# A vision layer on one core: row maxima taken over 256 keys straight into the FP16 stack, the stack's high parts written by ScalarE, the output division in one pass

## The reference

```python
h = _L0_tok_ref(x, L0_tok_W, L0_tok_b)
h = h + _L0_attn_ref(_layernorm(h, axis=-1), wq, wk, wv, wo)
h = h + _L0_ffn_ref(_layernorm(h, axis=-1), clip_x, clip_down, w_gate, w_up, w_down)
...
# attention, 16 heads of 16 features, 4 key/value heads, rotary positions
scores = jnp.einsum('bshd,bthd->bhst', q, k) * scale
scores = jnp.where(causal[None, None, :, :], scores, jnp.float32(-jnp.inf))
attn = jax.nn.softmax(scores, axis=-1)
out = jnp.einsum('bhst,bthd->bshd', attn, v).reshape(Bx, Sx, Dx)
return out @ wo
```

## Time and profile before

| | |
|---|---|
| median of 3 runs | 898.87 us (895.33, 898.87, 903.66) |
| span of the profiled execution, first to last instruction | 901.6 us |
| the profiled execution's own time | not listed apart; its span is 2.7 us above the median and within the runs |
| DVE busy over the span | 793.9 us (88%) |
| PE, POOL, ACT busy | 709.8, 537.5, 509.0 us |
| granted PE clock, mean | 0.938 of full |
| first stage | to about 724 us |
| second and third stage | about 724 us to the end |

### The profile page before, as it was taken

The page is one execution under the profiler, slowest core; times in us unless marked ns, Lnnn a source line. Parts: engine busy times, 40 slices in busy tenths (PEclk is TensorE's granted clock), DMA queues, the critical chain, the costliest instruction groups (busy, mean ns, idle before and its releaser), DMA issues. The chain is left out here.

```text
span 901.6 us, 21285 instructions
## 1 busy us (share of the span) xinstructions
PE 709.8 (79%) x6962; PEld 381.5 (42%) x6962; DVE 793.9 (88%) x1320; ACT 509.0 (56%) x748; POOL 537.5 (60%) x545
## 2 busy tenths in 40 slices
PE   3668788878888888888888888888786559996775
PEld 2444344444444444444444444444433223332453
DVE  6867688988999999999999999999996349998898
ACT  3324455555665565556655655565554438886664
POOL 1435666666777776677777766777753238882000
PEclk9686999999999999999999999999989769998999
DMA  7233445564554555555545555554544222223488
GB/s 255 64 70 84 99 106 117 119 126 103 132 119 108 120 118 120 122 128 134 119 108 120 118 121 122 126 135 90 92 89 86 50 44 50 47 47 105 137 261 254
DMA packets 245639, 102.86 MB, mean 114 GB/s; under 512 B 214496, under 2 KB 240864, under 8 KB 245600
## 3 DMA queue, kind: packets, MB, share of 16 engines
q1 hardware_dynamic: 245600, 102.37, 48.9%
HBM read 33.13 MB, written 16.78 MB: 55 GB/s over the span
## 5 line engine op out<-in xcount | busy, mean ns | idle before, releaser
L1199 DVE TENSOR_REDUCE act_all<-pair 128x8 f32<-128x1024 f32 x192 | 233.9, 1218 | 32.2 <-PE pair L551 23.2
L969 POOL TENSOR_SCALAR_AFFINE_SELECT act_all<-act_all 128x512 f32<-128x512 f32 x128 | 105.7, 836 | 104.0 <-ACT act_all L832 104.0
L832 ACT ACTIVATE act_all<-pair 128x768 f32<-128x768 f32 x128 | 104.0, 813 | 79.4 <-PE pair L568 79.4
L969 POOL TENSOR_SCALAR_AFFINE_SELECT ffn<-ffn 128x512 f32<-128x512 f32 x128 | 86.5, 676 | 97.6 <-ACT ffn L832 97.6
L832 ACT ACTIVATE ffn<-pair 128x768 f32<-128x768 f32 x128 | 102.6, 802 | 69.7 <-PE pair L568 69.6
L512 PE MATMUL pair<-act_all 128*128 128x256 f16 (+1 forms) x960 | 120.7, 281 | 5.0 <-POOL act_all L1007 3.3
L566 PE MATMUL pair<-act_all 64*128 64x256 f16 x512 | 74.3, 286 | 59.2 <-DMA act_all<-act_all 32.3
L544 PE MATMUL pair<-act_all 32*128 32x128 f16 x1536 | 78.3, 222 | 43.3 <-DMA act_all<-act_all 35.3
L512 PEld LDWEIGHTS pair<-act_all 128*128 128x128 f16 (+1 forms) x960 | 92.1, 100 | 31.2 <-issue 17.8
L1007 POOL TENSOR_TENSOR act_all<-act_all 128x1280 f16<-128x1280 f32 x31 | 82.5, 2660 | 17.9 <-ACT act_all L797 17.9
L544 PEld LDWEIGHTS pair<-act_all 32*128 32x128 f16 x1536 | 44.5, 94 | 89.9 <-issue 40.8
(11 more groups left out here) (130 smaller groups left out, 1500.8 us busy)
## 6 DMA issues: line engine op xcount, KB each, us to landing
act_all<-x_t SPq DMA_DIRECT2D x32, 640.0 KB, 4.2
out<-act_all SPq DMA_DIRECT2D x32, 256.0 KB, 2.6
ffn<-out SPq DMA_DIRECT2D x16, 512.0 KB, 4.7
out<-ffn SPq DMA_DIRECT2D x16, 512.0 KB, 3.2
act_all<-act_all SPq DMA_TRANSPOSE x192, 2.8
act_all<-w_down SPq DMA_DIRECT2D x1, 704.0 KB, 8.9
act_all<-w_emb SPq DMA_DIRECT2D x1, 640.0 KB, 3.8
ffn<-w_gate SPq DMA_DIRECT2D x1, 640.0 KB, 7.1
```

The costliest lines, as they stand in the source:

```text
L832: act.activation(probs[i // 4][:, o:o + 2, 0:3, :].rearrange("p h k s -> p h (k s)"), pair[1][:, :].rearrange("p (h c) -> p h c", h=2)[:, ...
L969: pool.affine_select(out=p, in_=p, pattern=[[0, 4], [1, P]], compare_op=ALU.is_ge, fill=0.0, base=0, channel_multiplier=-1).then_inc(maske ...
L1199: dve.tensor_reduce(to.rearrange("p (g k) -> p k g", g=GROUPS)[:, first:first + 2, :], pair[2][:, :].rearrange("p (k g t) -> p k g t", k=2 ...
```

## The change

- **Row maxima over 256 keys.** The second block's queries are now scored against all 256 keys at once. The six pairs are 0 and 1 (first block, all four groups of heads, as before) and 2 to 5 (second block, two groups of heads and two key heads each). A pair of 2 to 5 has four matmuls of 256 columns in place of eight of 128, and all six pairs get four mask matmuls (pairs 2 to 5 with 128 columns each in place of 256). The reduction of a pair still reads 1024 columns; for pairs 2 to 5 it gives 4 maxima, each over 256, in place of 8 over 128. It writes FP16 straight to column 48 of the stack. `merge_maxima` and `maxima_to_stack` are gone.
- **Scale.** ACT writes `max_stack` times 1/8, so that the rough scores come out already divided by 64.
- **Stack.** ACT fills the stack's high parts from `qk` in three ACTIVATEs (`fill_stack` on ACT, behind `exp_pair` 5): 640, 512 and 128 elements a partition. DVE's four COPYs are gone. `high` no longer waits for DVE; `low` on DVE waits for `stack_filled`, `add_rotated` on POOL too.
- **Output division.** One reciprocal of 32 and one multiplication of 512 over both banks, in place of two of 16 and two of 256.
- **Order on DVE.** `low` moves from before `norm_moments` to behind `peak_of`.

The diff, cut to its core:

```diff
+MAX_SCALE = 1.0 / 8.0
-UNIT_TILES = [(0, 0), (1, 0), (1, 1)]
...
             def turn_stack(n):
-                sp.wait_ge(stack_copied, n + 1)
+                sp.wait_ge(stack_filled, n + 1)
                 sp.wait_ge(low_ready, n + 1)
-                sp.wait_ge(max_ready, n + 1)
+                sp.wait_ge(unit_reduced, (n + 1) * PAIRS_U)
...
             def unit_pair(x, p):
+                else:
+                    for g in range(2):
+                        for j in range(2):
+                            kv = 2 * (p % 2) + j
+                            rows = slice(32 * kv, 32 * kv + 32)
+                            pe.matmul(max_bank[j][:, g * TOKENS:(g + 1) * TOKENS].rearrange("p (b t) -> p b t", b=TB),
+                                      max_op[rows, 1, 2 * (p // 2 - 1) + g, :], max_op[rows, :, 4, :], start=True,
+                                      stop=False, skip_group_check=True)
...
             def high(x):
-                wait(act, stack_copied, z.n)
-                wait(act, low_ready, z.n)
-                act.activation(max_stack[:, :, :, 0:16], qk[:, :, :, :], ACT.Copy).then_inc(high_ready, 1)
+                act.activation(max_stack[:, :, :, 0:16], qk[:, :, :, :], ACT.Copy, scale=MAX_SCALE).then_inc(
+                    high_ready, 1)
+            def fill_stack(x):
+                z = x + 2
+                stack = stacks[z.parity]
+                act.wait_ge(qk_ready, z.n + 1)
+                wait(act, first_turned[z.parity], z.half * 32)
+                wait(act, second_turned[z.parity], z.half * 32)
+                act.activation(stack[:, :, :, 16:32], qk[:, :, :, :], ACT.Copy)
+                act.activation(stack[:, :, 0:HEADS, 0:16], qk[:, :, 0:HEADS, :], ACT.Copy)
+                act.activation(stack[:, :, HEADS:QK, 32:48], qk[:, :, HEADS:QK, :], ACT.Copy).then_inc(stack_filled, 1)
...
             def low(x):
-                dve.wait_ge(high_ready, z.n + 1)
+                dve.wait_ge(stack_filled, z.n + 1)
...
             def reduce_pair(x, p):
+                to = stacks[y.parity][:, min(p // 2, 1), 0:HEADS, 48].rearrange("p (g k) -> p k g", g=GROUPS)
+                to = to[:, 2 * (p % 2):2 * (p % 2) + 2, :]
+                n_ = GROUPS
+                if p >= 2:
+                    to, n_ = to[:, :, 2 * (p // 2 - 1):2 * (p // 2 - 1) + 2], 2
                 dve.wait_ge(unit_scored, y.n * PAIRS_U + (p + 1))
-                dve.tensor_reduce(to.rearrange("p (g k) -> p k g", g=GROUPS)[:, first:first + 2, :],
-                                  pair[2][:, :].rearrange("p (k g t) -> p k g t", k=2, g=GROUPS), AX.X,
+                dve.tensor_reduce(to, pair[2][:, :].rearrange("p (k g t) -> p k g t", k=2, g=n_), AX.X,
                                   ALU.max).then_inc(unit_reduced, 1)
...
-            def o_sums(x, tb):
+            def o_sums(x):
...
+                o = pair[0][:, :].rearrange("p (b h d) -> p b h d", b=TB, h=HEADS)
+                dve.reciprocal(sums, o[:, :, :, HD:HD + 1]).then_inc(sums_ready, 1)
...
                 if (x + 1).exists():
-                    fill_stack(late)
                     reduce_pair(x, 5)
-                    merge_maxima(x)
-                    maxima_to_stack(x)
-                if (x + 2).exists():
-                    low(x)
                 if (x + 3).exists():
                     norm_moments(early)
                 if (x + -2).exists():
                     normalise2(late)
                     peak_of(late)
+                if (x + 2).exists():
+                    low(x)
                 if (x + -1).exists():
                     residual(x)
```

More of the change, by code:

```diff
@@ new lines, in unit_pair @@
+                halves = (slice(0, 64), slice(64, 128)) if p % 2 == 0 else (slice(64, 128), slice(0, 64))
+                for j in range(2):
+                    for t in halves:
+                        if p < 2:
+                            on_diagonal = max_bank[j][t, :].rearrange("p (g t) -> p g t", g=GROUPS)[:, :, t]
+                        else:
+                            on_diagonal = max_bank[j][t, :].rearrange("p (g b t) -> p g b t", g=2, b=TB)[:, :, 1, t]
+                        n_ = GROUPS if p < 2 else 2
+                        mm = pe.matmul(on_diagonal, eye_b[t, t],
+                                       tri_b[t, t].rearrange("p (a t) -> p a t", a=1).to_broadcast([64, n_, 64]),
+                                       start=False, stop=True, skip_group_check=True)
@@ L893, in step @@
                     exp_pair(late, 5)
+                if (x + 1).exists():
+                    fill_stack(late)
                 if (x + 3).exists():
@@ L997, in add_rotated @@
                 wait(pool, high_ready, z.n)
+                wait(pool, stack_filled, z.n)
                 wait(pool, low_ready, z.n)
@@ L1166, in low @@
                 stack = stacks[z.parity]
-                dve.wait_ge(high_ready, z.n + 1)
-                wait(dve, first_turned[z.parity], z.half * 32)
-                wait(dve, second_turned[z.parity], z.half * 32)
+                dve.wait_ge(stack_filled, z.n + 1)
                 fence(dve)
                 dve.tensor_tensor(stack[:, :, 0:HEADS, 32:48], qk[:, :, 0:HEADS, :],
-                                  max_stack[:, :, 0:HEADS, 0:16], ALU.subtract)
+                                  stack[:, :, 0:HEADS, 16:32], ALU.subtract)
@@ L1173, in low @@
                 dve.tensor_tensor(stack[:, :, HEADS:QK, 0:16], qk[:, :, HEADS:QK, :],
[L1174 to L1190 removed]
+                                  stack[:, :, HEADS:QK, 16:32], ALU.subtract).then_inc(low_ready, 1)
@@ L1343, in step @@
                 if (x + -1).exists():
[L1344 to L1347 removed]
+                    o_sums(x)
+                    o_normalise(x)
                 if (x + 1).exists():
```

82 lines of the change are left out of this document (17 added, 65 removed).

## The result

The changed kernel takes 850.69 us (median of 4 runs, 848.58 to 852.52), the kernel before 900.48 (4 runs, 895.33 to 903.66). The ratio is 0.946, 95% interval 0.942 to 0.950. The forecast was 870 in a range of 836 to 892: the direction and the range were right, but 29 us were forecast and about 50 came. The two profiled executions have spans of 846.9 and 901.6 us, so the rows explain 54.7.

The account below looks back on a forecast made before the run. The first stage was taken as bound by DVE, with PE's 16.8 us a step as floor. 24 steps at 1.0 us, 3 for the last three and 2 for the first steps give 29 us: 898.87 to 870, range 836 to 892.

Parts of the forecast that it names:

- The blocked TENSOR_SCALAR: DVE's `normalise2`: first TENSOR_SCALAR waits for a mask, second for all of POOL's `x_low` (2.66 us), ending at 417.65.
- Its meaning: DVE's step: of 4.1 us removed, three quarters is given back as waiting for POOL.
- Rival 1: Nothing blocks: `normalise2`'s TENSOR_SCALARs slip past before `x_low`, PE's loop decides, step 17.8 us, total 840; chance 0.25.
- The 0.44 us for low's second part: DVE's `low`: its second part can meet a POOL mask, taking 0.72 instead of 0.28 us, 0.44 more.
- 1.0 a step: First stage: gain taken per step, from a range of 0.8 to 1.25 us, making the step 19.1.
- 0.16 for PE: PE: new mask matmuls lengthen pair 2, between r1 and the next projection; 0.16 us a step taken off the gain.
- the patch matmuls' wait for the single division: PE: patch matmuls wait for the one output division on DVE and lose under 0.1 us.
- The lead-in and the first steps: Start of the first stage: 2 us gained, since first steps wait for PE and clock more than for DVE.
- ScalarE's load: ACT: three fill operations add 1.67 us a step, to near 68% busy, covered by the ended 2.9 us wait before `high`.
- PE's columns: PE: mask matmul columns equal in sum; four 256-column products replace eight of 128.
- Rival 2: ACT's fill costs its upper end, 2.5 us, exponentials come late, gain gone: 895 to 899; chance 0.12 with other small gains.
- Rival 3: PE's waits gather beyond about 2.2 us, its clock drops, each hit step costs 4.05 us: 908 to 919; chance 0.08.

Follow-up runs that it names:

- run 1: Changed kernel with POOL's `x_low` issued behind mask 7 instead of ahead of mask 5: 850.96 us, ratio 0.949 against the kernel before.
- run 3: Changed kernel with the output division in two parts, as before: 861.31 us, ratio 0.957 against the kernel before.
- run 4: Changed kernel with `low` back in its old place, ahead of the aggregates and `normalise2`: 883.59 us, ratio 0.983 against the kernel before.
- run 2: Kernel before with only POOL's `x_low` moved behind mask 7: 879.62 us, ratio 0.982.
- run 8: Changed kernel with the stack filled by DVE's four COPYs again, `high` waiting for them, factor of 8 left out: 888.08 us, ratio 0.990.
- run 10: Changed kernel with DVE's four COPYs filling the stack again, factor of 8 left out, and `x_low` behind POOL's last mask: 895.38 us, ratio 0.996.
- run 5: Changed kernel with `x_low` behind mask 7 and the output division in two parts: 851.15 us, ratio 0.948 against the kernel before.
- run 6: Kernel before with only the stack's high parts filled by ScalarE instead of DVE's COPYs: 900.65 us, ratio 1.003.
- run 12: Changed kernel with the stack filled by three DVE copies out of `qk` directly ahead of `low`: 907.36 us, ratio 1.006 against the kernel before.
- run 11: Kernel before with ScalarE filling the stack's high parts, `low` behind `peak_of`, and `x_low` behind POOL's last mask: 832.21 us, ratio 0.927.
- run 7: Kernel before with ScalarE filling the stack's high parts and `low` behind `peak_of`: 889.47 us, ratio 0.989.
- run 9: Kernel before with ScalarE filling the stack's high parts and `x_low` behind POOL's last mask: 904.86 us, ratio 1.006.

## Why the prediction was right, and where it was too small

**The blocked TENSOR_SCALAR**, the step on which the sum rested: right, to 0.2 us. Forecast: the mask first, then `x_low` for 2.66 us, the second TENSOR_SCALAR ending with it. Measured: 3.24 us for the two, ending at 417.84, `x_low` at 417.69. By the Trainium skill ("SBUF: State Buffer", section "SBUF: two separate sides") whichever of the two engines starts first has the port pair for the whole instruction; the rows fit that (3.24 us beside `x_low`, 0.93 in run 1 without it) and not a shared bandwidth.

**Its meaning** was only half right. I read the rest of the wait as a loss that could be won back, and Rival 1 as what would happen without it. Run 1 took the wait away and gained nothing: PE's list is by now as long. A wait on the busiest engine is worth no more than the distance to the next path, here 0.1 us.

**The 0.44 us for low's second part**: not met in the middle of the changed kernel, met in run 3. The forecast's 1.0 a step lay between 0.8 with that mask and 1.25 without it, that is 0.97 and 1.41, each less 0.16 for PE. Measured are 1.47 without the mask (20.06 less 18.59) and 0.98 with it (run 3, whose even steps are 19.08). Both are the forecast's figures before the 0.16 is taken off, so PE's extra work does not show in the step, and the mask makes the rest of the difference. Why it is missed: the term that I put at "under 0.1 us", the patch matmuls' wait for the single division, is 0.60 us, against 0.18 in run 3. That delays PE by 0.4, so the exponential and the mask behind it. The mask then starts at 419.28, together with `low`'s second part, and now it is the mask that stands (0.78 us against 0.63 to 0.68). The changed kernel shows the other case too: while its wait for the division is 0.42 to 0.44 us (to 150 us), L1194 takes 0.71 to 0.72 and two full steps are 18.9 us long; from 166 us on the wait is 0.6 and L1194 0.28. What moved it from one to the other was not tried. So the two steps of the working that failed here are one: PE's wait for the division was mis-sized, and the mask on `low` hung on it.

**The lead-in and the first steps**: forecast 2 us for the first and 1.0 a step for the next ones, measured 14.6 and 11.3 (the forecast had 4 for these four steps). This is the term that was mis-sized most: 12.6 and 7.3, so 20 of the 26 us missing; the twenty steps in the middle bring 7 more (27.2 against 20), the end 1 less. Before, `high` (L825) stood 6.93 us and was let go by the COPYs. They took 4.31 us there instead of 1.99, beside POOL's addition (to 59.46) and `x_low` (59.42 to 62.08). `qk` itself was ready at 59.46, so the COPYs cost `high` 3.1 of the 6.93. Then PE's granted clock was 0.50 for 16 us. After, `high` (L833) goes when `qk` is ready, 3.8 us earlier. First the kernel before, DVE, ACT and the windows:

```profile
58.13 4.31 DVE L1186 COPY act_all<-act_all 128x512 f16<-128x512 f16 x4
```

```profile
62.61 0.74 ACT L825 ACTIVATE act_all<-act_all 128x640 f16<-128x640 f32 x1 [6.93 <-DVE act_all L1186]
```

```profile
66.00:74.00 8.00, 5.82 (x47) 2.52 (x48) 3.62 (x6) 1.02 (x3) 1.31 (x2) 0.50 0.68 168
74.00:82.00 8.00, 7.18 (x47) 3.62 (x47) 5.11 (x6) 4.52 (x6) 6.06 (x6) 0.50 0.18 35
```

and the changed kernel:

```profile
58.78 0.74 ACT L833 ACTIVATE act_all<-act_all 128x640 f16<-128x640 f32 x1 [3.82 <-POOL act_all L1024]
```

```profile
66.00:74.00 8.00, 5.71 (x50) 2.27 (x47) 5.21 (x7) 4.97 (x8) 5.28 (x6) 0.79 0.49 132
74.00:82.00 8.00, 6.70 (x77) 3.79 (x74) 3.73 (x7) 5.18 (x10) 6.76 (x7) 1.00 0.44 85
```

The runs bear this out in part. The clock can't be put down to `high` alone: between 50 and 58 us, before `high` goes, it was already 0.63 in the kernel before and 1.00 in the changed one, and in runs 3 and 4, where `high` waits for no COPY, it is 0.50 from 74 to 82 us as well. In the four profiles in which `high` waits for COPYs (before, runs 2, 8 and 10) the first residual is at 105.4 to 110.1. In the ten in which it doesn't, it is at 98.7 to 105.9, and at 102.7 or more in five of them (runs 3, 4, 5, 6 and 12). On the mean (107.0 against 102.1) freeing `high` is worth some 5 us there, and several more hang on how PE's clock falls out in one execution; with one profile of each kernel these can't be parted. The 11.3 us of the next four steps are dips of the clock too: before, two of the four were 22.15 and 24.1 us long (from 153.82 and from 195.94), with a clock of 0.92 and 0.86 behind waits of PE of 2.68 and 2.67 us for a transpose; after, none of the four is above 19.0, and the one dip comes a step later. I had left these dips in the forecast as if they stayed. No run was made to show why they went.

**ScalarE's load**: right. The three operations are 0.73, 0.62 and 0.30 us, 1.65 together (forecast 1.67), ACT is at 70.5% (forecast 68), `high` waits for DVE no more, and the fill lies beside other work, as long as `low` stands late. Run 4 shows its price where it doesn't: 2.81 us a step on DVE. The move of `low`, which I priced only as 0.81 us that come between, is what makes the fill pay: without it the change is 883.59, with it 850.69. DVE, forecast at over 95% busy, is at 93.66.

**PE's columns**: wrong, by little. I took the columns to be equal in sum, and they are, but the work is not. Four masks of 256 columns take 0.41 us, four of 128 take 0.30, not half:

```profile
405.33 0.30 PE L561 MATMUL pair<-act_all,eye_b 64*64 64x128 bf16 x4
```

So PE does 17.1 us a step (92.10% of 18.60) instead of 16.8. In the forecast only 0.16 of it stood. Run 11 against run 5, which differ in the maxima alone, puts the whole price at 0.6 us a step (17.9 against 18.5): 0.3 of it is PE's own work. The rest is more waiting, among it 0.37 us a step for the turned output in front of L617 (4.1 in 11), which run 11's list of waits does not have; what makes that transfer late was not tried.

**The rivals.** Rival 1 named 17.8 us for a step in which nothing blocks. The changed kernel did not reach it where `x_low` was out of the way (18.5 in runs 1 and 5), but the old list of PE does: run 11 has 17.9, and its 832 us stand near the rival's 840. Rival 2 did not come. Rival 3's mechanism came in runs 6, 7 and 12, where PE waited 1.7 to 2.7 us at once and the clock of 100 us fell to 0.90 to 0.97. In run 9 it is 0.97 to 1.00 in spite of waits of 2.2 us, and the time goes into the waits themselves. In the changed kernel it came once: PE waits 1.52 us for a transpose at 196.82, and that step is 20.7 us long. Between 200 and 560 us its longest wait is 0.6.

**How much was luck.** 850.69 lies below the forecast's own neighbourhood of 855 to 885. It is in the range because the range was drawn down to 836 for rival 1, and rival 1 did not come. The working is 20 us too small at the start of the stage, and nothing in it foresaw that part. Two slips of the working change nothing: "15.9 us" for DVE is the step less 4.1, and DVE's own 19.3 less 4.1 is 15.2; and r5 takes 1.24 to the next start (414.93 to 416.17 in the earlier trace rows), not 1.15, but the mask of 414.18 runs in either case.

## What to carry to other kernels

When several edits free the same engine, don't price them one by one: what each removed here was partly waiting, and the waiting moved to the next instruction of the same kind. Before you drop an instruction, ask what then arrives first beside the long operation of the other engine, and whether something on the way to the bounding engine hangs on it; and before building a new form of the work to dodge such a wait, try to move the long operation, and look at what it meets in its new place (run 9). Moving `x_low` and `low` and filling by ScalarE gave 67 us (832.21), the whole change 50.

## What was not expected of the hardware

A TENSOR_SCALAR of two numbers a partition stands as long as a large one: L1238 of run 9 takes 2.18 us beside `x_low` and 0.16 alone (the row is with run 9).

And a delay can gain: the 0.4 us that PE waits longer for the single division moved a mask off `low` and made the kernel about 10 us faster (run 3 against the changed kernel).

The reductions cost the same in either form. With four FP16 numbers out, strided, they take 1.22 us; with eight FP32 numbers they took 1.21 to 1.22.
